# Where global attention turns its maxima and outputs, and when a block's first value product comes

## What is computed

```python
q = rope((x @ Wq).reshape(b, s, 32, 8)).transpose(0, 2, 1, 3) * 8 ** -0.5
k = rope((x @ Wk).reshape(b, s, 32, 8)).transpose(0, 2, 1, 3)
v = (x @ Wv).reshape(b, s, 16, 16).transpose(0, 2, 1, 3)
probs = softmax(einsum('bhqd,bhkd->bhqk', q, k)).reshape(b, 16, 2, s, s)
w = probs[:, :, 0] - lam * probs[:, :, 1]
attn = einsum('bhqk,bhkd->bhqd', w, v)
attn = attn * rsqrt(mean(attn ** 2) + 1e-5) * subln_g * (1 - LAMBDA_INIT)
x = x + attn.reshape(b, s, 256) @ Wo
```

## Time and profile before

| | |
|---|---|
| runs | 8448.02, 8451.05, 8458.74 us (median 8451.05) |
| profiled execution, span from first to last instruction | 8446.8 us |
| TensorE, VectorE, ScalarE, GpSimd busy | 91%, 82%, 75%, 38% |
| granted TensorE clock, mean | 0.960 |
| global attention in the first pair | 327 to 980 us |

### The profile page before, as it was taken

One profiled execution on the slowest core, in us unless ns is written; L12 is line 12 of the kernel. 1 busy time (PEld: TensorE's weight loads), 2 busy tenths in 40 slices (PEclk: granted clock), 3 DMA queues, 4 the chain that ended last, 5 costly groups with the idle time before them and its releaser, 6 DMA issues. The chain is left out here.

```text
span 8446.8 us, 166394 instructions
## 1 busy us (share of the span) xinstructions
PE 7668.1 (91%) x65600; PEld 2778.4 (33%) x65600; DVE 6929.7 (82%) x8963; ACT 6349.5 (75%) x11710; POOL 3201.4 (38%) x4546
## 2 busy tenths in 40 slices
PE   6899988999889998899988999889998999989999
PEld 3322343223432234322343223432234322343223
DVE  5899768997689976899768997689966899668996
ACT  3699756997569975699756997569975699756996
POOL 3244232442334423344233442334423344233441
PEclk9999999999999999999998999999999999989999
DMA  0100001000010000100001000010000100001000
GB/s 30 46 21 22 18 11 46 21 25 15 11 46 22 24 15 11 46 25 21 15 12 46 24 21 15 11 50 21 25 16 6 50 21 25 20 3 50 25 21 21
DMA packets 219183, 205.49 MB, mean 24 GB/s; under 512 B 108086, under 2 KB 143414, under 8 KB 218358
## 3 DMA queue, kind: packets, MB, share of 16 engines
q1 hardware_dynamic: 218364, 194.46, 8.0%
HBM read 123.83 MB, written 67.37 MB: 23 GB/s over the span
## 5 line engine op out<-in xcount | busy, mean ns | idle before, releaser
L1467 DVE TENSOR_REDUCE mfull<-ps 128x1 f32<-128x1024 f32 x4096 | 4708.3, 1217 | 331.9 <-PE ps L1389 331.1
L1542 ACT ACTIVATE work<-ps 128x512 f32<-128x512 f32 x8192 | 4406.7, 598 | 371.5 <-PE ps L1411 255.2
L1429 PE MATMUL ps<-work,vbuf 128*32 128x256 f32 x32768 | 2623.5, 392 | 119.5 <-ACT hh L1562 119.5
L1389 PE MATMUL ps<-kop,qop 48*128 48x512 bf16 x8192 | 2490.0, 386 | 48.8 <-DVE mfull L1467 23.7
L1411 PE MATMUL ps<-qop,kop 51*128 51x512 bf16 x8192 | 2487.6, 384 | 0.4 <-DMA qop<-mT 0.2
L1429 PEld LDWEIGHTS ps<-work,vbuf 128*32 128x32 f32 x32768 | 654.3, 108 | 1767.9 <-issue 966.8
L1411 PEld LDWEIGHTS ps<-qop,kop 51*128 51x128 bf16 x8192 | 481.8, 93 | 1639.4 <-ACT work L1542 1525.0
L1493 POOL CAST mpart<-mfull 128x16 bf16<-128x16 f32 x256 | 50.5, 197 | 2472.0 <-issue 2005.6
L253 POOL TENSOR_TENSOR rstd<-rstd,nhalf 128x8 f32<-128x8 f32 x64 | 109.2, 1707 | 1644.4 <-DVE rstd L247 1644.4
L445 POOL TENSOR_TENSOR hh<-work,hmask 128x1024 f32<-128x1024 f32 x256 | 521.0, 2062 | 447.4 <-POOLq L1663 329.0
L1511 POOL TENSOR_TENSOR work<-work,none 128x16 f32<-128x16 f32 x224 | 650.8, 2906 | 17.9
(11 more groups left out here) (185 smaller groups left out, 9042.3 us busy)
## 6 DMA issues: line engine op xcount, KB each, us to landing
qop<-scratch SPq DMA_DIRECT2D x512, 64.0 KB
scratch<-work SPq DMA_DIRECT2D x32, 768.0 KB, 4.1
scratch<-hh SPq DMA_DIRECT2D x32, 768.0 KB, 3.6
kop<-scratch SPq DMA_DIRECT2D x256, 96.0 KB
vbuf<-in_x SPq DMA_DIRECT2D x9, 2048.0 KB, 8.3
qop<-scratch SPq DMA_DIRECT2D x512, 32.0 KB
kop<-scratch SPq DMA_DIRECT2D x256, 64.0 KB
qop<-mT SPq DMA_DIRECT2D x1024, 3.0 KB
```

The costliest lines, as they stand in the source:

```text
L1389: pe.matmul(ps[:, b + n, :], qop[r:r + KQ, s, i, t * P:(t + 1) * P], kop[r:r + KQ, s, i, half(n)], start=True, stop=True).then_inc(s_ms, 1)
L1429: mm = pe.matmul(ps[VW * i:VW * (i + 1), OB, cols], vp[:, b, t, (G * gl + i) // 2, :], prob[:, u % PS, i, cols], start=t == 0 and part == ...
L1467: v.tensor_reduce(mfull[:, m // CUT % 2, r // ROWS * G // 2 + i, to:to + 1], ps[:, b:b + NB, :].rearrange("p b n -> p (b n)"), AX.X, ALU.m ...
L1542: act.activation(prob[:, u % PS, hl, :], ps[:, EB[slot % len(EB)], :], ACT.Exp, scale=scale).then_inc(s_ex, 1)
```

## The change

The turned maxima and the early turns both take slots of the ring `EB`. `EXTRA` lists the steps with such a slot, behind the step's two exponentials. The maxima turn stays in step 11 but writes into the ring, so that it waits for ACT's release of a bank and no longer for DVE, and `max_scores` no longer waits for ACT's copy. Each early turn becomes two halves of two transposes, in steps 7 and 14 behind the scores; POOL's normalising starts after the second. The first value product of a block moves from step 3 to step 4, which now has both parts (`value_step`).

```diff
-            EARLY = [STEPS * (g + 1) + o for g in range(FIRST) for o in (9, 25)]
+            HALVES = [STEPS * (g + 1) + o for g in range(FIRST) for o in (7, 14, 23, 30)]
+            MAXIMA = [CUT * (h + 1) - 1 + TURN - AHEAD for h in range(NB * GROUPS)]
+            EXTRA = sorted(HALVES + MAXIMA)
...
             def slot_of(k):
 
-                return k + turns_until(k // NB)
-
-            def turn_slot(j):
-
-                return NB * EARLY[j] + j
+                return k + sum(1 for s in EXTRA if s < k // NB)
+
+            def extra_slot(step):
+
+                return NB * max(step + 1, 0) + EXTRA.index(step)
...
-                m = CUT * (h + 1) + TURN
-                return m, ps[0:PARTS * CUT, max_bank(m), 0:P // 2].bitcast(BF16)
+                return ps[0:PARTS * CUT, EB[maxima_slot(h) % len(EB)], 0:P // 2].bitcast(BF16)
...
-            def tile_due(e, part):
-
-                u = (e - 3 - part) // 2
-                return u if (e - 3 - part) % 2 == 0 and 0 <= u < GROUPS * NB * T else None
+            def value_step(u, part):
+
+                return 2 * u + 4 if u % T == 0 else 2 * u + 3 + part
...
-                        if m % CUT == TURN and n == 0 and m >= CUT:
-                            pe.wait_ge(s_mts, m // CUT)
...
                     def turn_maxima(h):
                         pe.wait_ge(s_mc, CUTS * (h + 1))
-                        m, turned = turn_at(h)
-                        pe.wait_ge(s_mr, min(m - 1, LAST))
-                        pe.transpose(turned, mpart[:, :, :, :].rearrange("p h s t -> p (h s t)"),
-                                     identb[:, :]).then_inc(s_mt, 1)
+                        bank_for(maxima_slot(h))
+                        pe.transpose(turn_at(h), mpart[:, :, :, :].rearrange("p h s t -> p (h s t)"),
+                                     identb[:, :]).then_inc(s_sc, 1)
...
-                    def early_turn(j):
+                    def early_half(j, part):
                         pe.wait_ge(s_oe, NB * (j // 2 + 1))
-                        turned_heads(pe, bank_for(turn_slot(j)), j // 2, j % 2).then_inc(s_sc, 1)
+                        bank = bank_for(half_slot(j, part))
+                        for t in range(T // 4):
+                            at = (j % 2 * T // 2 + part * T // 4 + t) * P
+                            mm = pe.transpose(ps[:, bank, t * P:(t + 1) * P], oT[:, j // 2 % NG, at:at + P],
+                                              ident[:, :])
+                        mm.then_inc(s_sc, 1)
...
-                        if e == 0:
+                        if e == EXTRA[0]:
                             pe.wait_ge(s_ve, TT // 2)
-                        if e in EARLY:
-                            early_turn(EARLY.index(e))
                         for n in range(NB):
                             if 0 <= e < LAST:
                                 exp_scores(NB * e + n)
                             if e + AHEAD < LAST:
                                 max_scores(e + AHEAD, n)
-                        if at(e, TURN) is not None:
-                            turn_maxima(at(e, TURN))
-                        for part in range(2):
-                            if tile_due(e, part) is not None:
-                                values(tile_due(e, part), part)
+                        if e in MAXIMA:
+                            turn_maxima(MAXIMA.index(e))
+                        if e in HALVES:
+                            early_half(HALVES.index(e) // 2, HALVES.index(e) % 2)
+                        for u, part in values_due(e):
+                            values(u, part)
...
-                        if e in EARLY:
-                            early(EARLY.index(e))
+                        if e in HALVES and HALVES.index(e) % 2:
+                            early(HALVES.index(e) // 2)
```

More of the change, by code:

```diff
@@ L1262, in diff_attention @@
             s_mc = sem("da_mc")
-            s_mt, s_mts = sem("da_mt"), sem("da_mts")
             s_sc, s_ex, s_pv, s_oe = sem("da_sc"), sem("da_ex"), sem("da_pv"), sem("da_oe")
@@ L1291, in exp_tile, with half_slot, maxima_slot @@
                 return u, u // (NB * T), u // T % NB, u % T, hl
-            def turns_until(e):
-                return sum(1 for s in EARLY if s <= e)
             def slot_of(k):
-                return k + turns_until(k // NB)
-            def turn_slot(j):
-                return NB * EARLY[j] + j
+                return k + sum(1 for s in EXTRA if s < k // NB)
+            def extra_slot(step):
+                return NB * max(step + 1, 0) + EXTRA.index(step)
+            def half_slot(j, part):
+                return extra_slot(HALVES[2 * j + part])
+            def maxima_slot(h):
+                return extra_slot(MAXIMA[h])
             def max_bank(m):
@@ L1326, in at, with values_due @@
                 return m // CUT if m % CUT == CUT - 1 and 0 <= m < LAST else None
-            def tile_due(e, part):
-                u = (e - 3 - part) // 2
-                return u if (e - 3 - part) % 2 == 0 and 0 <= u < GROUPS * NB * T else None
+            def value_step(u, part):
+                return 2 * u + 4 if u % T == 0 else 2 * u + 3 + part
+            def values_due(e):
+                near = range(max(0, (e - 4) // 2), min(GROUPS * NB * T, (e - 3) // 2 + 1))
+                return [(u, part) for u in near for part in range(2) if value_step(u, part) == e]
             with nc.Block() as block:
@@ L1353, in maxima @@
                         for n in range(NB):
-                            sp.wait_ge(s_mts, NB * g + n + 1)
+                            sp.wait_ge(s_ex, maxima_slot(NB * g + n) + 1)
                             for side in range(2):
@@ L1446, in _ @@
                                 max_scores(e + AHEAD, n)
-                        if at(e, TURN) is not None:
-                            turn_maxima(at(e, TURN))
-                        for part in range(2):
-                            if tile_due(e, part) is not None:
-                                values(tile_due(e, part), part)
+                        if e in MAXIMA:
[4 more added lines that the diff above has]
+                            values(u, part)
                         if e in LATE:
                             if e == LATE[0]:
-                                pe.wait_ge(s_mts, NB * GROUPS)
+                                pe.wait_ge(s_mr, LAST)
                                 pe.wait_ge(s_oe, NB * (FIRST + 1))
@@ L1491, in cut @@
                         if h >= 1:
-                            pool.wait_ge(s_mt, h)
+                            pool.wait_ge(s_sc, maxima_slot(h - 1) + 1)
                         link(pool.tensor_copy(mpart[:, :, 0, :], mfull[:, s]))
@@ L1507, in link @@
                             pool.wait_ge(s_ch, done[0])
-                        pool.wait_ge(s_ex, turn_slot(j) + 1)
+                        pool.wait_ge(s_ex, half_slot(j, 1) + 1)
                         y = raw[j % 2]
@@ L1543, in exponentials, with keep_half @@
                                        ACT.Exp, scale=scale).then_inc(s_ex, 1)
-                    def keep_raw(j):
-                        slot = turn_slot(j)
-                        if j >= 2:
+                    def keep_half(j, part):
+                        slot = half_slot(j, part)
+                        if j >= 2 and part == 0:
                             act.wait_ge(s_ch, LINKS * (j - 2) + 2)
                         act.wait_ge(s_sc, slot + 1)
-                        src = ps[:, EB[slot % len(EB)], :].rearrange("p (k w) -> p k w", w=VW)
-                        act.copy(raw[j % 2], src[:, :, 0:LD + 1]).then_inc(s_ex, 1)
+                        src = ps[:, EB[slot % len(EB)], 0:HALF // 2].rearrange("p (k w) -> p k w", w=VW)
+                        keys = slice(part * DH // 4, (part + 1) * DH // 4)
+                        act.copy(raw[j % 2][:, keys], src[:, :, 0:LD + 1]).then_inc(s_ex, 1)
                     def keep_maxima(h):
-                        act.wait_ge(s_mt, h + 1)
+                        act.wait_ge(s_sc, maxima_slot(h) + 1)
                         if h >= 1:
                             act.wait_ge(s_md[(h - 1) // NB % SLOTS], placed(h - 1))
-                        act.copy(mT[:, :], turn_at(h)[1]).then_inc(s_mts, 1)
+                        act.copy(mT[:, :], turn_at(h)).then_inc(s_ex, 1)
                     def keep_output(u):
@@ L1565, in _ @@
                     for e in CLOCK:
-                        if e in EARLY:
-                            keep_raw(EARLY.index(e))
                         if 0 <= e < LAST:
@@ L1570, in _ @@
                                 exponentials(NB * e + n)
[L1571 to L1574, removed]
+                        if e in MAXIMA:
+                            keep_maxima(MAXIMA.index(e))
+                        if e in HALVES:
+                            keep_half(HALVES.index(e) // 2, HALVES.index(e) % 2)
+                        for u, part in values_due(e):
```

(2 more changed lines are left out.)

## The result

The change makes the kernel faster: 8407.57 us (median of 4 runs) against 8450.81, a ratio of 0.995 with a 95% interval of 0.9935 to 0.9964. The forecast was 8441, in a range of 8360 to 8480, with 0.40 for faster. The gain of 43 us is four times the 10 us of my sum.

The account below looks back on a forecast made before the run. TensorE, busy 91% of the span, was taken to set the ordinary step. Terms of -9.0, +1.8, +6.5 and -0.6 made -1.3 us a pair, -10 over eight: 8441 us, range 8360 to 8480.

Parts of the forecast that it names:

- The first turn: A pair's first turn waits 0.62 us for VectorE and leads the first exponentials; forecast -0.6 us a pair.
- The covers: GpSimd's maxima cut stays ahead of TensorE; its early-turn chain, now after step 14, stays covered by some 3 us.
- The turn of the maxima: Step 11: the VectorE wait goes, bank waits take part back; gain 0.30 us, 30 times, -9.0 us a pair.
- the seam: Steps 3 and 4, where a new output block begins; the prediction read 0.56 us extra in step 3.
- S + 0.95: S starts a step's first score product; its second exponential, d, was read as beginning 0.98 or 0.91 us later.
- the d of step 12: Step 12's second exponential: its bank expected free 1.67 us after step 11's start, a wait of 0.18 us.
- my three places: Steps 9, 11 and 3, with 0.58, 0.63 and 0.56 us extra per 16 steps; sum 1.77 of 1.80.
- The halves: Early turns: two halves make 0.65 us for 0.58, 28 times 0.065, +1.8 us a pair.
- The later value product: Steps 3 and 4 of a block: a late bank makes it 0.21 us slower, 31 times, +6.5 us a pair.
- The signs that I had named: Expected in the profile: blocks 19.45 us apart, step 12's second exponential at 1.67, 0.8 us between step 4's exponentials.
- The rival of partly free banks: Ring banks partly free: 0.40 at the turn, +0.15 at the block, 8400; chance 0.22 together with never-late banks.
- their slack stays as it is: DMAs of the maxima: copy about 0.5 us later, but steps until use gain 0.3 and 0.18, so slack unchanged.

Follow-up runs that it names:

- the last experiment: Maxima's turn moved behind step 11's value products, against the kernel with ring maxima, whole early turns, later value product and moved block copy: 8315.53 us, ratio 0.9843.
- the halves alone: Only the early turns split into halves, against the kernel before the change: 8500.13 us, ratio 1.0062.
- the maxima alone: Only the maxima turned in the exponentials' banks, early turns whole, value product in step 3, against the kernel before: 8337.82 us, ratio 0.9872.
- the two fastest kernels: Whole change without halves, block's copy between step 3's exponentials: 8320.55 us; the same with the maxima's turn behind the value products: 8315.53 us.

## Why the prediction was right, and where its sizes were wrong

The direction and the mechanisms held: each part did what the sum says, two of three cost time, and the banks of the ring are what is late next. Two terms were right as they stood. The first turn was forecast at -0.6 us a pair, and the lead went from 27.0 to 26.3. The covers held too: the cut of the maxima ends 0.57 us before the turn in a steady period (642.11, 642.68), and GpSimd is idle for 3.4 us before that cut. Three sizes were wrong.

- **The turn of the maxima**, -0.30 us a period: measured -0.43. The failing number is "TensorE goes on 0.13 us after an end on ScalarE", which I used for every wait. I took it from the value product behind the copy of a block. It depends on the instruction that waits:

```profile
633.02 0.63 ACT L1551 ACTIVATE work<-ps 128x512 f32<-128x512 f32 x1
633.70 0.39 PE L1416 MATMUL ps<-qop,kop 51*128 51x512 bf16 x1 [0.19 <-ACT work L1551]
...
641.95 0.59 ACT L1551 ACTIVATE work<-ps 128x512 f32<-128x512 f32 x1
642.68 0.22 PE L1402 MATMUL ps<-identb,mpart 128*48 128x128 bf16 x1
```

  Both wait for an exponential. The d in the seam starts 0.05 us after its end (633.65 to 633.70), the turn of the maxima 0.14 after its own (642.54 to 642.68), and a half turn of outputs 0.14 as well. In the trace an instruction of TensorE's sequencer that only waits (EVENT_SEMAPHORE, 0.05 us) stands ahead of the turn, the half turn and the product behind the copy, and none ahead of the d. That this makes the difference is not shown.

  And I put the d of the exponentials at S + 0.95, between two kinds of step; in step 11 it is the early kind. Its bank is then free at 0.42 + 0.49 + 0.60 + 0.05 = S + 1.56 and not 1.67. Since the d of step 12 would go at 1.54 anyway, a wait of 0.18 shrank to 0.02. Against that the turn went at S + 0.60 and not 0.56, so step 12 started at 1.32 and not 1.27. And the old kernel lost 0.03 us in step 12 (643.51 to 644.65) that I had left out; it is also what the 1.77 of my three places lacks to 1.80.
- **The halves**, +0.065: measured +0.19. I shared out the 0.58 us of four transposes in proportion. The upper bound from the group of two in the output stage was the better value. By the Trainium skill ("TensorE: Matmul & The Clock Gate", Part 4: PE-mode transpose) the estimate for a group of two was 0.38 us. The trace has 0.34 and 0.36, so each group has 0.10 to 0.14 us that do not shrink with it (twice 0.34 less 0.58, twice 0.36 less 0.58), less than the page's access latency of 173 ns. The page measured bf16, and these transposes are fp32. The 0.07 us by which step 7 waits for its bank were in no term.
- **The later value product**, +0.21: measured +0.05. Two errors: the same 0.13 (d at S3 + 1.49, not 1.57), and 0.52 + 0.57 for two parts in a row, where the trace has 634.02 to 635.02, 1.00 us. The tail's 2.10/4 is not how two parts run in the middle.

The total came out inside the range in part by luck. The turn and the later value product were each forecast 0.13 and 0.16 us a period too dear, the halves 0.13 too cheap, and one of these errors cancels another. My "588 us of 620" for VectorE mixes two windows (the rows are of 327 to 980, 653 us); nothing hangs on it. The signs that I had named were off with the sizes: blocks 19.33 us apart and not 19.45, the d of step 12 at S11 + 1.56 and not 1.67, and 0.98 us from c to d in step 4 (632.72, 633.70) and not 0.8.

By the measured sizes, 0.425, 0.19 and 0.05, the same sum gives 30 x -0.425 + 28 x 0.19 + 31 x 0.05 - 0.6 = -6.5 us a pair, against 5.4 us measured. The rest lies in single periods of the traces: three longer ones (below) cost 0.63 us where before one cost 0.11, the first block of the second pair gains 0.06 us instead of 0.37, and its last two blocks lose 0.26, of which the sum has 0.10. That makes 1.0 of the 1.1 us. The rival of partly free banks, 8400, was closer than my forecast: it had the turn right (0.40), but the halves at the wrong size and the block too dear.

## What to carry to other kernels

In a ring of buffers a borrowed slot can make its borrower wait, and the user two slots later. Here the turn waited 0.07 us for its bank, the d of step 12 0.02, and when the turn moved behind the value products (the last experiment) the d waited those 0.07 instead. Work out when such a buffer is free from waits of the same kind of waiting instruction: 0.05 and 0.14 us after the same kind of release decided here whether a wait existed. A wait that is worked out as a small difference of two long times is uncertain by its own size: 0.18 us, between 1.67 and 1.49, came out as 0.02. And when a change has three parts, forecast each: here one part carried 113 us, and two gave back 65.

## What the runs showed that I had not expected

- The DMAs of the maxima come close to being late. In a steady period, the last one landed this long before the step that reads it (the median, from the semaphore updates in the traces): 0.52 us before the change, 0.45 after it, 0.88 with the halves alone, 0.09 with the maxima alone, and 0.09 and 0.10 in the two fastest kernels. TensorE's product never started less than 0.05 us after a landing. So my sentence that their slack stays as it is held for the whole change, where the half turn in step 14 gives them time; without the halves the slack is nearly used up. What the fastest kernels could still gain between step 11 and the end of a block is at most some 0.04 us a period (an estimate, 0.09 less 0.05).

  With the maxima alone one such DMA did come late, once a pair: a block of 19.75 us against 19.08. Its last transfer landed 2.51 us after its issue and not 1.78. TensorE waited at the start of the next block:

```profile
640.02 0.39 PE L1416 MATMUL ps<-qop,kop 51*128 51x512 bf16 x1 [0.61 <-DMA qop<-mT]
```

  After the change one block of the first pair has such a wait, 19.43 against 19.33. What these transfers collide with was not tried.
- Other long periods are no DMA waits. In the first pair after the change, 19.62 and 19.59 us against 19.33 are a step 7 and a step 11 in which d and then the turn waited for their banks. In both ScalarE had paused for 0.36 us a step earlier; in the first it was here:

```profile
481.86 2.06 ACT L1551 ACTIVATE work<-ps 128x512 f32<-128x512 f32 x4 [0.36 <-PE ps L1416]
```

  The score that it is said to wait for had started at 481.09. The same two periods are longer with the halves alone (19.98 and 19.90 against 19.70), and before the change one step 7 is (19.63 against 19.51). They stand at the same place in every pair. What makes ScalarE pause is open.
- The granted clock in the first pair (0.50 or 0.96 from 327 to 352 us) goes with starts that differ by 3 us between two kernels that are the same up to there. From pair to pair of one execution the start-to-start time varied by up to 8 us, so it takes periods within a stage, and not the totals, to see 0.05 us.
